# Mamba and mixture-of-experts layer on one core: the time steps dt reach the 128 state rows through memory instead of by 16 on-chip copies

## The reference, cut to what matters

```python
dt = softplus(ts @ dt_proj_w.T + dt_proj_b)            # [token, channel], 1024 channels
def step(state, inp):                                  # one token after the other
    dA  = exp(dt_t[..., None] * A)                     # channel x 16 states
    dBx = dt_t[..., None] * B_t[:, None, :] * x_t[..., None]
    state = state * dA + dBx
    y = einsum('bds,bs->bd', state, C_t)
```

## Time and profile before

| what | us |
|---|---|
| three timed runs: median (lowest to highest) | 1344.96 (1337.76 to 1350.12) |
| the profiled execution: its own time | 1337.05 |
| its span in the profile | 1335.2 |

### The profile page before, as it was taken

One profiled execution on the slowest core, in us unless ns is written; L12 is line 12 of the kernel. 1 busy time (PEld: TensorE's weight loads), 2 busy tenths in 40 slices (PEclk: granted clock), 3 DMA queues, 4 the chain that ended last, 5 costly groups with the idle time before them and its releaser, 6 DMA issues.

```text
span 1335.2 us, 53004 instructions
## 1 busy us (share of the span) xinstructions
PE 1233.3 (92%) x21558; PEld 796.7 (60%) x21558; DVE 1078.3 (81%) x1235; ACT 894.6 (67%) x1925; POOL 866.8 (65%) x456
## 2 busy tenths in 40 slices
PE   6999999399999999999899998999999999999998
PEld 4777767255555555555555554455555678787876
DVE  5989888489999979899899987899999564646554
ACT  4766667287897977978878897678777243424343
POOL 3445467188989979899889997889989340303030
PEclk9999999699999989999999998999999999999999
DMA  8364554779999989999999999899898843122130
GB/s 269 122 261 160 180 207 143 244 213 283 296 302 281 319 251 274 298 282 321 281 258 316 275 309 283 260 280 290 255 325 260 282 182 139 51 102 87 63 125 31
DMA packets 131714, 305.90 MB, mean 229 GB/s; under 512 B 18400, under 2 KB 22752, under 8 KB 129824
## 3 DMA queue, kind: packets, MB, share of 16 engines
q1 hardware_dynamic: 124048, 286.18, 65.8%
q0 software_dynamic: 7600, 18.91, 7.1%
HBM read 214.04 MB, written 57.69 MB: 204 GB/s over the span
## 4 chain that ended last, share of the span: by engine, by line
PE 37%; ACT 11%; DMA 8%; DVE 8%; issue 8%; SPq 6%; ACTq 1%; POOL 1%; DVEq 0%; POOLq 0%
PE p_dBx L1392 7%; PE p_dBx L1334 7%; DVE state L1023 5%; SPq L851 5%; ACT dA L1173 4%; DMA xt_for_dtx<-xt_d 4%; PE p_y L1343 3%; PE p_g L1320 3%; DMA dt_blocks_odd<-step_rows 3%; PE p_y L1403 3%; PE p_g L1403 2%; PE p_u L1403 2%; PE p_dt L1403 2%; PE p_u L1303 2%; PE p_g L1303 2%
## 5 line engine op out<-in xcount | busy, mean ns | idle before, releaser
L1023 DVE TENSOR_TENSOR_SCAN state<-dA,state_carry,p_dBx 128x512 f32<-128x512 f32 x512 | 617.7, 1261 | 44.4 <-PE p_dBx L1334 42.2
L959 POOL TENSOR_TENSOR h_times_C<-state,C_bcast 128x1024 f32<-128x1024 f32 x128 | 305.0, 2388 | 62.5 <-DVE state L1023 60.9
L959 POOL TENSOR_TENSOR C_bcast<-state,C_bcast 128x1024 f32<-128x1024 f32 x128 | 315.9, 2611 | 20.4 <-DVE state L1023 19.3
L1334 PE MATMUL p_dBx<-B_diagonals,step_rows 64*32 64x128 f32 x16384 | 295.3, 275 | 29.2 <-DVE state L1023 20.1
L1334 PEld LDWEIGHTS p_dBx<-B_diagonals,step_rows 64*32 64x32 f32 x16384 | 233.2, 106 | 142.3 <-issue 140.6
L1173 ACT ACTIVATE dA<-dt_blocks_odd,A_par 128x512 f32<-128x512 f32 x256 | 169.4, 709 | 40.5 <-DMA dt_blocks_odd<-step_rows 40.5
L1173 ACT ACTIVATE dA<-dt_blocks_even,A_par 128x512 f32<-128x512 f32 x256 | 169.4, 709 | 29.5 <-DMA dt_blocks_even<-step_rows 29.5
L288 POOL TENSOR_TENSOR w_in_parts_lo<-C_bcast,w_in_parts_hi 128x512 fp32r<-128x512 f32 x64 | 96.2, 1504 | 95.2 <-ACT w_in_parts_hi L505 94.9
L973 POOL TENSOR_TENSOR step_rows<-step_rows 128x512 f32<-128x512 f32 x16 | 22.0, 1407 | 181.8 <-DMA step_rows<-moe 181.8
L384 DVE SCALAR_TENSOR_TENSOR conv_out<-conv_in,conv_w,conv_out 128x512 f32<-128x512 f32 x96 | 107.4, 1127 | 16.2 <-ACT conv_out L529 13.9
L1303 PE MATMUL p_g<-w_gate_pair,step_rows 128*64 128x352 f32 x512 | 85.0, 473 | 9.4 <-ACT step_rows L1184 9.1
(11 more groups left out here) (185 smaller groups left out, 2062.3 us busy)
## 6 DMA issues: line engine op xcount, KB each, us to landing
w_gate_pair<-in_w_gate SPq DMA_DIRECT2D x32, 1408.0 KB
w_up_pair<-in_w_up SPq DMA_DIRECT2D x32, 1408.0 KB
w_down_pair<-in_w_down SPq DMA_DIRECT2D x66, 512.0 KB
dt_blocks_odd<-step_rows SPq DMA_DIRECT2D x256, 64.0 KB
dt_blocks_even<-step_rows SPq DMA_DIRECT2D x240, 64.0 KB
w_down_pair<-in_w_down SPq DMA_DIRECT2D x33, 384.0 KB
g_d<-y_gated SPq DMA_DIRECT2D x33, 256.0 KB, 3.8
sz_d<-silu_gate SPq DMA_DIRECT2D x32, 256.0 KB, 2.2
```

Source lines behind the costliest of these rows:

```text
L959: pool.tensor_tensor(hc[m][:, b, :, :], hb[:, q, :, :], Cb[:, NM * (c % 2) + GS * m:NM * (c % 2) + GS * m + GS, :], ALU.mult).then_inc(s_h ...
L1023: ins = dve.tensor_tensor_scan(hb[:, g % NBUF, s, :], dA[:, g % NBUF, s, :], pB[:, g % 2, :].rearrange("p (t s) -> p s t", s=GS)[:, s, :], ...
L1334: ins = pe.matmul(out[DB * p:DB * p + DB, half, j, :, :], dtxT[k, j * P + DB * b:j * P + DB * b + DB], diag[k, ND * cp + 2 * j + p // 2, a ...
```

## The change

`take_dt` moves from group 5 to group 4 on ACT, ahead of the Exp of the expert gate. `spread_dt` no longer copies SBUF to SBUF. It issues four stores, one per block, into a new buffer in device memory, `dt_d` (2 x 32 x 4 x 512 numbers, one half per parity of the step). SP then waits until all four have landed. Then it issues four loads, one per quarter; each brings the whole 256 KB half, so that each of 32 partitions gets one row of 4 x 512 numbers, 8 KB. The semaphores now count quarters: ACT waits at group 0 for all four, where before it waited at each of groups 0 to 3 for one block. `take_dt` waits for the stores of the step before (they read `dts`) and no longer for the copies.

```diff
-WEIGHT_AT, SOFTPLUS_AT, SILU_AT, DT_COPY_AT, DIAG_AT = 2, 3, 4, 5, 6
+WEIGHT_AT, SOFTPLUS_AT, SILU_AT, DT_COPY_AT, DIAG_AT = 2, 3, 4, 4, 6
...
                 sp.wait_ge(s_dtc, n + 1)
                 for b in range(NB):
-                    for p in range(NB):
-                        sp.dma_start(dtr[n % 2][DB * p:DB * p + DB, b, :], dts[DB * b:DB * b + DB, :]).then_inc(s_dtr[b], 16)
-
-            for b in range(NB):
-                sp.sem_inc(s_dtr[b], 16 * NB)
+                    sp.dma_start(io["dt_d"][n % 2][:, b, :], dts[DB * b:DB * b + DB, :]).then_inc(s_dts, 16)
+                sp.wait_ge(s_dts, 16 * NB * (n + 1))
+                for p in range(NB):
+                    sp.dma_start(dtr[n % 2][DB * p:DB * p + DB, :, :], io["dt_d"][n % 2]).then_inc(s_dtr[p], 16)
+
+            for p in range(NB):
+                sp.sem_inc(s_dtr[p], 16)
+            sp.sem_inc(s_dts, 16 * NB)
...
-            def take_dt(n, used):
+            def take_dt(n, stored):
 
                 act.wait_ge(s_dtx, n + 1)
-                if used is not None:
-                    for b in range(NB):
-                        act.wait_ge(s_dtr[b], used)
+                act.wait_ge(s_dts, stored)
                 act.activation(dts, pM[:, :], ACT.Copy).then_inc(s_dtc, 1)
...
-                            if g < NB:
-                                act.wait_ge(s_dtr[g], 16 * NB * i + 16 * NB)
+                            if g == 0:
+                                for p in range(NB):
+                                    act.wait_ge(s_dtr[p], 16 * i + 16)
```

More of the change, by code:

```diff
@@ L780, in stages2and3 @@
             sem("dt_ready"), sem("dt_copied"))
-        s_dtr = [sem(f"dt_block{b}_loaded") for b in range(NB)]
+        s_dtr, s_dts = [sem(f"dt_quarter{p}_loaded") for p in range(NB)], sem("dt_stored")
         s_dtx, s_dxTps, s_dxT = sem("dtx_ready"), sem("dtxT_in_psum"), [sem(f"dtxT_ready{h}") for h in range(2)]
@@ L903, in _ @@
             sp.wait_ge(s_gst, 16 * (STEPS + 3))
-            for b in range(NB):
-                sp.wait_ge(s_dtr[b], 16 * NB * STEPS)
+            for p in range(NB):
+                sp.wait_ge(s_dtr[p], 16 * STEPS)
             sp.wait_ge(s_sc, 16 * (STEPS + 4))
@@ L1568 @@
     for name, shape in (("xn_d", (ROWS, XS)), ("moe", (2 * ROWS, H)), ("xt_d", (STEPS, P, CH)), ("sz_d", (STEPS, P, CH)),
-                        ("g_d", (STEPS + 1, P, CH)), ("bc_d", (2 * NS, T)), ("ts_d", (NCH, R3, CH)), ("wdt_d", (R3, ND, P)),
+                        ("g_d", (STEPS + 1, P, CH)), ("bc_d", (2 * NS, T)), ("ts_d", (NCH, R3, CH)), ("wdt_d", (R3, ND, P)), ("dt_d", (2, DB, NB, CH)),
                         ("xnT_d", (NCH, P, KH, CH))):
```

## The result

The changed kernel takes 1357.38 us (median of 20 runs, 1351.24 to 1364.8); the kernel before, timed beside it, 1345.93 us (20 runs, 1337.76 to 1355.76). The ratio is 1.0089, interval 1.0069 to 1.0109. So the change costs 11.5 us. The direction was forecast, the size was not: 52 us over the median were forecast, four to five times too much. By the forecast's own yardstick (1%, 13 us, as the least that counts as a change) the outcome is "same", to which it had given a chance of 0.12. The time lies in its range, 1340 to 1450 us, only because that range reached down to rival C; rival A's 1380 to 1440 missed it.

A forecast was written before the change was run, and what follows sets the result against it. The DMA queue, 0.95 busy, was taken to bound the recurrence: 22.9 + 1.2 + 1.8 = 25.9 us a step against 24.1, +56 us over 31 steps, 1393; half of 7.9 us on top gave 1397 us, range 1340 to 1450.

The forecast's parts named there:

- rival C: Nothing changes: ACT's lead hides the longer way and the scatter fills the gap, or gain balances loss; 1332 to 1358, chance 0.12.
- rival A: The forecast itself, in the recurrence: the DMA queue pays for the change; 1380 to 1440 us, chance 0.70.
- Sum by the queue: DMA queue work per recurrence step: 22.9 + 1.2 + 1.8 = 25.9 us; low end 24.1, high end 27.1.
- Sum by the loop: Way of dt from first exponential through stores and loads to the next: 11.7 + 5.5 + 7 = 24.2 us a step.
- The earlier copy: On ACT, dt's copy comes up to 1.67 us earlier; gains nothing where the queue is what is late.
- SP's issues: 8 issues plus the wait for stores replace 16 on SP: about as before, priced at zero, bounds -1 and +1 us.
- Traffic of the loads: Loads of 1.05 MB into 32 partitions move at the on-chip copies' rate: 4.9 us a step, lower bound 2.6.
- rival B: Loads of 8 KB rows run at full rate, 2.6 us instead of 4.9; 1306 to 1314 us, chance 0.13.
- The round trip: Queue gap between the stores' last byte and the loads' first: 1.8 us a step, bounds 0 and 1.8.
- Rival D: The queue does not drain: stores wait behind the weights, loads come on top; 1457 to 1490 us, chance 0.05.
- signs that I had named for A: Profile after: fewer steps, ACT's wait over 70 us, loads about 218 GB/s, 1.5 to 2 us hole, DVE waiting for Ln.

The follow-up runs named there:

- e2: Kernel before with only the copy of dt moved from group 5 to group 4, the 16 on-chip copies kept: 1337.29 us, ratio 0.9891.
- light queue: Changed kernel with the experts' down weights loaded once instead of in every step: 1342.62 us, ratio 1.0055.
- both relieved: Changed kernel with the down weights loaded once and the gate weights issued behind the loads of dt: 1320.38 us, ratio 0.9795.

## Why the prediction was right in sign and wrong in size

**The step that failed** is "Sum by the queue", and in it the term of the queue's work, 22.9 + 1.2, which I called "a bound that no order of work escapes". Measured, the work of a step is 0.91 x 24.8 = 22.6 us, stores and loads in it; 24.1 had been forecast. The idle of the queue came out near the forecast: 24.8 less 22.6 is 2.2 us, where I had 1.8. The miss is thus 25.9 - 24.8 = 1.1 us a step, 34 us in 31 steps, which is the whole distance between the +56 forecast for the profiled execution and the +21.6 it shows.

Two things were wrong in that term. First, a share of 0.95 was read as work that must be done. Share times step, for the very transfers of the kernel before in other orders, is no constant: 0.95 x 24.09 = 22.9 us before, 0.93 x 23.94 = 22.3 us with the early copy, 0.88 x 24.93 = 21.9 us with the gate weights behind the copies as well (the windows of these two runs, columns as the earlier trace rows):

```profile
262.00:1010.00 748.00, 715.27 (x18594) 391.97 (x18596) 682.35 (x655) 621.08 (x1444) 663.15 (x310) 0.99 0.93 284
```

```profile
262.00:1010.00 748.00, 673.60 (x17908) 376.22 (x17896) 648.06 (x625) 598.68 (x1397) 637.40 (x296) 0.99 0.88 272
```

So the share counts time for which the engines held packets, and up to 1 us of it per step came and went with the order of the work alone. The untouched traffic of q0 took 16 us less in the changed kernel. That the 16 copies on chip were what held it up is not shown: in the changed kernel with its loads in halves, which has none of these copies either, q0 took 6.7% of 1367.1 us, 91.6 us. Secondly, the bytes of the stores were priced as if each us of queue were a us of the step. Four stores of 64 KB and four of 2 KB cost the same (1.0226 and 1.0223), and one store for four changes nothing (1.0111 against 1.0089, intervals overlapping).

**The "Sum by the loop" came nearer.** It gave 11.7 + 5.5 + 7 = 24.2 us; the trace shows 12.0 + 5.5 + 7.3 = 24.8. It misses by 0.6 us, the queue's sum by 1.1 on the other side. By the loop alone I would have forecast next to nothing (24.2 against 24.1), a time within 1% of what came. I had both sums and took the larger. That the loop's sum came so near is in part luck: its rule that a us of the way of dt is a us of the step failed twice, with the copy late (some 40 us expected, 1.0075 measured) and with the loads in halves. The experiments show that in the changed kernel neither sum is the answer alone: 24.4 us for the way of dt with a light queue, 24.4 for the full queue with the gate weights out of the way, and 23.66 with both relieved.

**The earlier copy.** Priced at 0 to 1.67 us and then subtracted in the loop only. In the changed kernel it is worth nothing (1.0075 without, 1.0089 with it); in the kernel before it is worth 1.1 to 1.35%. PE also has a wait that I had not listed, 22.8 us over the stretch. Line 1186 is ACT's copy of the experts' transposed tokens from `p_u`, at group 2, ahead of the softplus parts and of the copy of dt:

```profile
L1305 PE MATMUL p_g<-w_gate_pair,step_rows 128*64 128x352 f32 x480 | 79.6, 475 | 23.0 <-ACT step_rows L1186 22.8
```

It was 9.1 us before, and 1.7 in the on-chip kernel with the early copy (e2). In the changed kernel with the late copy it is the same as with the early one:

```profile
PE p_g L1305 <- ACT step_rows L1186: 22.6, 23, 1.2
```

So the earlier place of the copy does not make PE wait. The wait goes with ACT's stand for dt at the head of the step: 22.8 us where ACT stands 119.7, 6.5 where it stands 79.6 (no wait for the stores), 2.0 where it stands 55.4 (both reliefs).

**SP's issues** were priced at zero, bounds -1 and +1 us. The trace: from the first store's issue to the sz load's 7.33 us (719.70 to 727.03), before 10.11 (708.87 to 718.98), so SP gets there 2.8 us sooner in the steps shown. I had taken 5 to 9 us for the stores' landing; the loads were issued 4.9 us after the first store, 5.4 in the mean. That this is worth something I had missed: the x tile is on time in the changed kernel with either place of the copy.

**Traffic of the loads.** Taken at the rate of the copies, 4.9 us for 1.05 MB, against rival B's 2.6. The windows show 199 to 238 GB/s at full share, that is 4.4 to 5.3 us. Right, and B is out.
**The round trip.** Priced at a hole of 1.8 us: measured 1.8 us at a share of 0.10 in the step shown, and POOL's scatter does not fill it. The split into completion and start holds too: the last bytes move at about 723.6 us, the loads are issued at 724.58, their first bytes move after 725.5. The section of the Trainium skill, DMA: Bandwidth & Descriptors, that the forecast names for 2.0 us describes transfers issued by GpSimd. These are issued by SP, and no run here shows that figure for them. ACT's wait was to be clearly over 70 us in nearly every step: 119.7 in 30 of 30. DVE was to lose the x tile's waits and to wait for Ln: 18.6 to none, 8.2 to 15.1. The signs that I had named for A are all there. They are signs of the round trip; A's other term, more work for the queue, did not come. Rival D (the queue does not drain) is out: the hole is there in the step shown. Rival C is the nearest in time, 1357.4 at the top of its 1332 to 1358. Of its reasons one is wrong, as the scatter does not fill the gap; gain and loss in balance is in part what happened, with SP's shorter list on the one side and the round trip on the other.

The Trainium skill, DMA: Bandwidth & Descriptors, Rules for kernel authors, would have small transfers coalesced, and puts the mark at 64 KB. Here 16 of just 64 KB became 4 of 256 KB and 4 of 64 KB, and the kernel is 0.9% slower. A gain by fewer transfers is there in SP's shorter list; what decides is the dependent pair of transfers that came with it.

## What to carry to other kernels

A busy share of the DMA queue near 1 is not a sum of work that can be added to. Where a sum by the queue and a sum by the way of the data both come near the step, take neither as a bound, and expect that what is won in one comes back in the other until both are relieved, as it did here. A hop through memory costs two things that no share shows: the wait of the issuing engine for the landing (here 3.7 us a step), and the dry queue after it (some 1.8 us). Split a change that has two parts before judging it, and try each part with and without the other: here the earlier copy gained over 1% with the copies on chip and nothing through memory, and the way through memory cost 0.75% with the late copy and 2% with the early one.

## What the runs showed of the hardware that was not expected

- Issue time depends on the kind of transfer. A copy of 64 KB from SBUF to SBUF takes SP 591 ns to issue, a store of 64 KB to memory or a load of 256 KB from it 422 ns, a store of a single row 256 ns at the median of 124.
- SP can be the scarce engine with its list of issues alone. Four issues more (1.35 us in the step shown, of 24.7) cost 2.2% where SP had 16 copies to issue, and nothing that can be measured where it gets to the same point 2.8 us sooner.
- The time that the queue takes for the same packets changes with what runs beside them: 18.91 MB of POOL's gathers and scatters took 94.8 us of 16 engines before, 78.7 after and 91.6 with the loads in halves; all transfers of the kernel before took 22.9 us of the queue per step, and 21.9 in another order.
- A 64 KB store under a full queue lands 2.6 to 7.3 us after its issue, median 4.1, and the median tells little: with ACT's copy 1.66 us later, the wait behind it was 1.53 us shorter.
